# Low-part work of an MLP moved behind the steps of a search, a residual sum by tiles, and a last store in two pieces

## The chip, the cores and the metric

The kernel runs on one core of a Trainium2 chip. The metric is the device time of one execution in microseconds (us). TensorE (PE) does the matmuls and transposes; VectorE (DVE), ScalarE (ACT) and GpSimd (POOL) do the rest; SyncE (SP) issues nearly all DMA transfers. Each engine runs its own instructions in order, and they wait for each other by semaphores.

## The reference

```python
def _L0_cond_ref(emb_s, emb_t, attention_weights, k):
    ...
    att = jax.nn.softmax(attention_weights, axis=-1) * (1.0 / np.sqrt(n).astype(np.float32))
    adj = adj * att
    adj = adj.at[:, diag, diag].set(-jnp.inf)
    _, idx = jax.lax.top_k(flat, k)
    out = jnp.zeros((g, n * n), dtype=adj.dtype).at[rows, idx].set(1.0)
...
def _L1_cond_ref(x, timestep_embed, ada_w, ...):
    ...
    attn_out = attn_out @ out_w + out_b
    x = x + gate1 * attn_out
    x2 = _ln(x) * (1.0 + scale2) + shift2
    h = jax.nn.gelu(x2 @ ffn_w1 + ffn_b1, approximate=False)
    x = x + gate2 * (h @ ffn_w2 + ffn_b2)
    return x
x = x + _L0_cond_ref(fside_BxSx1_0, cond_2048[:, None, :], x, 5120)
x = x + _L1_cond_ref(x, cond_2048, L1_cond_ada_w, ...)
```

x has 4 sequences of 512 rows by 512 columns, in float32. For each, a 0/1 mask of the 5120 largest of 512 x 512 products is added to x; then a transformer block (16 heads of 128, MLP width 2048, modulated by cond) is applied, and its output, which holds x already, is added to x once more. So the result holds the masked x twice.

## The kernel before

Every float32 product is made of three passes with operands split into a high and a low part (`mm3`, lines 1118 to 1120: high by high, high by low, low by high). A tile of MLP-in or a group of four chunks of MLP-out is 12 matmuls of 512 columns. A high part is written by ScalarE, its low part by VectorE.

The four sequences run one after the other. The 5120th largest value of sequence b + 1 is found by bisection while sequence b is computed: 32 steps, each a count by VectorE (`count`, line 803) and one by ScalarE (`topk_count`, line 584) of half the elements, their total by two one-column matmuls of TensorE (`take_total`, lines 1125 and 1126), and the move of the candidate by VectorE (`topk_move`, lines 857 and 860). The search for sequence 0 stands alone at the start; sequence 3 has none beside it. `SLOTS` places the steps: 11 under the heads, 5 under the output projection, then one behind tile 3 of MLP-in and one behind each later tile but tile 12 (11 of them), and the last four at the places (0,0) to (0,3) of MLP-out. At such a place TensorE takes the total (`between`), VectorE makes the step (`step_at`) and ScalarE the next count (`next_count`). (u, r) of MLP-out is unit u, chunks 4r to 4r + 3.

MLP-in has 16 tiles f. The first four are made together in two halves of the rows; from f = 4 on each takes one PSUM bank of seven in turn and waits for the gelu of tile f - 7 (`h_hi`). ScalarE applies the gelu twice (line 751 into `tmp`, which holds four tiles; line 753 into the high part of `act`), and VectorE subtracts (`hidden_lo`, line 995). Before, both loops have, for tile f, first the step of its place, then ScalarE gelu f and VectorE low part f - 1. Unit 0 of MLP-out, which follows, takes the hidden tiles as its 16 chunks and waits for their low parts (`h_lo`): chunk 12 for low parts up to 14, chunk 15 for 15.

VectorE's residual sum `x2 += xm` (line 1062, all four row tiles in one instruction) stands between the second layer norm and the loop of MLP-in. After unit 3 of MLP-out `mlp_add` adds the last column block, and SyncE stores all of `x2` (line 421). Gated outputs of units 1 and 2 (line 990) are transposed by TensorE at place (3,1) (line 1238).

In sequence 0 alone the weights are split too, 40 halves: ScalarE copies the high half (line 622), GpSimd subtracts for the low one (line 514). Both halves of unit 9, which is unit 1 of MLP-out, are copied near the end of MLP-in and in MLP-out, `split_unit(b, 6 + f // 4, 0)` behind gelu 15 and `split_unit(b, 9 + u, 1)` at r = 1. The step at place (0,3) ends with the marks of equal elements (`eqm`, line 874); GpSimd and VectorE then have the splits and the mask (lines 880 to 888) side by side.

Of the kernel before, what the change touches and what calls it, by code (L numbers as in the profile page):

```python
# [40 lines left out]
ALU = mybir.AluOpType  # L41
# [3 lines left out]
P = 128  # L45
# [115 lines left out]
def before_in_place(n, among):  # L161

    return sum(m in among for m in range(n) if PLACE[m] == PLACE[n])


def is_first(b):
# [4 lines left out]
def block_kernel(nc, x, cond, weights, ada_w, cols, out):  # L171
    ctx = ExitStack()
    with ctx:
# [139 lines left out]
        def wait_apart(eng, signal, value):  # L313


            eng.wait_ge(signal, value)
            eng.sem_inc(waits_met, 1)
# [32 lines left out]
        def _(sp):  # L350
# [68 lines left out]
            def store(b):  # L419
                wait_apart(sp, out_ready, b + 1)  # L420
                sp.dma_start(seq(out_seq, b), x2[:, :, :].rearrange("p i d -> p (i d)"))\
                    .then_inc(out_stored, 16)

            def first_sequence():
                load_raw(2, AHEAD + 2)
                wait_apart(sp, xm_ready, 1)
                load_x(1)
                for i in range(DESKS):
                    sp.wait_ge(desk_saved[i], 16 * len(range(i, len(PRE), DESKS)))
                for n in PRE:  # L430
                    if n in (v_half(1, 0), v_half(1, 1)):
                        load_ahead(n, v_done, QUAD)
                load_raw(AHEAD + 2, AT[unit_half(3, 0)])
                wait_apart(sp, pt_done, H * NT)
                load_x_again(1)
                load_raw(AT[unit_half(3, 0)], AT[unit_half(9, 0)] + 2)
                for u in (6, 7, 8):
                    for half in range(2):
                        load_ahead(unit_half(u, half), f_done, 4 * (u - 5))
                load_raw(AT[unit_half(9, 0)] + 2, NHALF)  # L440
                save_split(NHALF - 2)
                save_split(NHALF - 1)
                for place in PLACES:
                    sp.wait_ge(w_saved[place], 16 * w_credit(place))
# [38 lines left out]
            for b in range(1, B - 1):  # L483
                sequence(b)
            sequence(B - 1, last=True)
            store(B - 1)
            sp.wait_ge(out_stored, 16 * B + STORE_CREDIT)


        @block.gpsimd  # L490
# [80 lines left out]
        def _(act_e):  # L571
# [137 lines left out]
            def sequence(b, last=False):  # L709
                split_qk(b, 0)  # L710
                split_qk(b, 1)
                for idx in range(3):
                    v_part(b, idx)
                qk_part(b, 0)

                nc.scalar.activation(table[:, :], ident[:, 0:1], ACT.Exp)
                split_v(b, 1, 0)
                v_part(b, 3)
                for h in range(H):
                    head(b, h, last)  # L720

                def next_count(place):
                    step = SLOTS.get(place)
                    if not last and step is not None:
                        if step + 1 < STEPS:
                            topk_count(b + 1, step + 1)
                        else:
                            topk_sides(b + 1)

                split_unit(b, 2, 0)  # L730
                next_count(("out", 1, 2))
                next_count(("out", 1, 3))
                split_unit(b, 2, 1)
                for r in range(4):
                    if r % 2 == 0:
                        split_unit(b, 3, r // 2)
                    next_count(("out", 2, r))
                split_unit(b, 4)
                ln_root(b * LNS + 1, 0, NT // 2)
                ln_hi(b * LNS + 1, ada2[:, C:2 * C], ada2[:, 2 * C:3 * C], ROWS[0])  # L740
                split_unit(b, 5, 0)
                ln_root(b * LNS + 2, NT // 2, NT)
                ln_hi(b * LNS + 2, ada2[:, C:2 * C], ada2[:, 2 * C:3 * C], ROWS[1])
                split_unit(b, 5, 1)
                for f in range(KC):
                    next_count(("mlp_in", f // 4, f % 4))
                    act_e.wait_ge(f_done, b * KC + (f + 1))
                    if f >= 4:
                        act_e.wait_ge(h_lo, b * KC + (f - 3))
                    bk = bank[BANKS["mlp_in"][f % TURNS]]  # L750
                    nc.scalar.activation(tmp[:, f % 4, :], bk[:, :], ACT.Gelu,
                                         bias=col("b1", f)).then_inc(g_done, 1)
                    nc.scalar.activation(act[:, 0, f, :], bk[:, :], ACT.Gelu,
                                         bias=col("b1", f)).then_inc(h_hi, 1)
                    if f % 4 == 3:
                        split_unit(b, 6 + f // 4, 0)
                    elif f % 4 == 1 and f > 4:
                        split_unit(b, 5 + f // 4, 1)
                for u in range(4):
                    for r in range(4):  # L760
                        next_count(("mlp_out", u, r))
                        if r == 1 and u < 3:
                            split_unit(b, 9 + u, 1)
                        elif r == 3 and u < 2:
                            split_unit(b, 10 + u, 0)
                            if u == 1 and not last:
                                ln_root(b * LNS + LNS)
                        elif not last and (u, r) in ((2, 3), (3, 1)):
                            split_v(b + 1, 0, u - 2)
                if not last:  # L770
                    ln_hi(b * LNS + LNS, ada1[:, 0:C], ada1[:, C:2 * C])
# [24 lines left out]
        def _(dve):  # L796
# [201 lines left out]
            def sequence(b, last=False):  # L998
# [10 lines left out]
                def step_at(place):  # L1009
                    if not last and place in SLOTS:  # L1010
                        topk_step(b + 1, SLOTS[place])
# [17 lines left out]
                def attn_add(u, half=0):  # L1029
# [2 lines left out]
                        return add_back(u, xm)  # L1032
                    return add_back(u, xm, half * NT // 2, (half + 1) * NT // 2)

                def mlp_add(u):
                    dve.wait_ge(y2_back, b * C + (u + 1))
                    return add_back(u, x2)
# [5 lines left out]
                for r in range(4):  # L1043
                    step_at(("out", 2, r))
                    if r in (1, 2):
# [13 lines left out]
                modulate_lo(b * LNS + 1, ROWS[0])  # L1059
                normalise(b * LNS + 2, x2, 1, NT // 2, NT)  # L1060
                modulate_lo(b * LNS + 2, ROWS[1])
                V.tensor_tensor(x2[:, :, :].rearrange("p i d -> p (i d)"),
                                x2[:, :, :].rearrange("p i d -> p (i d)"),
                                xm[:, :, :].rearrange("p i d -> p (i d)"), ALU.add)
                for f in range(KC):
                    step_at(("mlp_in", f // 4, f % 4))
                    if f:
                        hidden_lo(b, f - 1)
                hidden_lo(b, KC - 1)
                for u in range(4):  # L1070
                    for r in range(4):
                        if u and r == 0:
                            mlp_gate(u - 1)
                        step_at(("mlp_out", u, r))
                        if (u, r) == (1, 2):
                            mlp_add(0)
                        if u == 3 and r == 0:
# [360 lines left out]
```

## Time and profile before

| | us |
|---|---|
| median of 3 runs | 1700.54 (1699.61 to 1701.47) |
| profiled execution, its own time | 1700.58 |
| its span, first to last instruction | 1698.7 |
| TensorE busy | 1615.8 (95%) |
| VectorE busy | 1159.3 (68%) |
| ScalarE busy | 856.8 (50%) |
| GpSimd busy | 158.0 (9%) |

Between the span and the execution's time lie 1.9 us. Rows of a timeline give start and duration in us, engine, line, operation, output and inputs, and in brackets the time for which the engine stood before it and what released it. Starts of successive instructions can lie closer than their durations, since an engine's pipeline overlaps them.

### The profile page before, as it was taken

Reading aid. Unit: us, or ns where it says so; the run is one execution under the profiler, and the core shown is the slowest. Engines: PE = TensorE matmul, PEld = TensorE weight load, DVE = VectorE, ACT = ScalarE, POOL = GpSimd, SP = SyncE. Lnnn points to the kernel's source line nnn. Section 1 sums busy time; section 2 is a strip of 40 time slices with the busy share of each in tenths; the row PEclk is TensorE's granted clock in tenths of the full one; section 3 lists DMA queues with packets and bytes.
Section 4 is the critical chain, followed back from the end, with each engine's and each line's share of the span. In section 5 each row is a group of like instructions: output and inputs, shape, how many; then the busy total and the mean of one; then the engine's idle time right before and its main releaser. Section 6 shows DMA issues by size and latency. Waiting matters only on the chain.

```text
span 1698.7 us, 22501 instructions
## 1 busy us (share of the span) xinstructions
PE 1615.8 (95%) x8268; PEld 1354.3 (80%) x8268; DVE 1159.3 (68%) x2524; ACT 856.8 (50%) x1623; POOL 158.0 (9%) x89
## 2 busy tenths in 40 slices
PE   1869999999999999999999999999999999999998
PEld 1758888888788888888778888888878888888887
DVE  6767877767785887776774887776675666665421
ACT  4546666654835455553743555554572445444240
POOL 5511312214040000000000000000000000000000
PEclk9999999999999999999999999999999999999999
DMA  9803525536566232324355232134344331332453
GB/s 373 303 32 124 186 80 180 186 135 251 197 217 236 79 120 101 110 105 157 149 198 221 84 125 114 61 124 149 149 165 186 145 125 50 125 123 85 164 198 124
DMA packets 63853, 256.32 MB, mean 151 GB/s; under 512 B 4352, under 2 KB 4480, under 8 KB 60800
## 3 DMA queue, kind: packets, MB, share of 16 engines
q1 hardware_dynamic: 63456, 254.56, 40.7%
q8 instruction: 66, 1.08, 0.2%
q10 hardware_dynamic: 288, 0.33, 0.1%
q14 instruction: 43, 0.35, 0.1%
HBM read 200.34 MB, written 54.53 MB: 150 GB/s over the span
## 4 chain that ended last, share of the span: by engine, by line
PE 86%; DVE 9%; ACT 3%; issue 1%; DVEq 1%; DMA 0%; SPq 0%; ACTq 0%
PE bank L1118 25%; PE bank L1120 24%; PE bank L1119 24%; PE bank L1212 6%; DVE tb L803 3%; PE bank L1238 1%; PE bank L1280 1%; PE bank L1275 1%; PE bank L1142 1%; PE bank L1276 1%; DVE prob L971 1%; PE bank L1160 1%; ACT prob L679 1%; PE bank L1164 1%; PE bank L1161 1%
## 5 line engine op out<-in xcount | busy, mean ns | idle before, releaser
L1118 PE MATMUL bank<-xT,w 128*128 128x512 f32 x704 | 280.5, 398 | 0.5 <-POOL w L514 0.5
L679 ACT ACTIVATE prob<-bank,nbias 128x512 f32<-128x512 f32 x256 | 176.6, 690 | 201.0 <-DVE nbias L968 201.0
L1120 PE MATMUL bank<-xT,w 128*128 128x512 f32 x704 | 274.8, 390 | 0.0
L1119 PE MATMUL bank<-xT,w 128*128 128x512 f32 x704 | 274.5, 390 | 0.0
L1118 PE MATMUL bank<-act,w 128*128 128x512 f32 (+1 forms) x576 | 217.6, 378 | 0.8 <-DVE act L932 0.8
L1120 PE MATMUL bank<-act,w 128*128 128x512 f32 (+1 forms) x576 | 211.0, 366 | 0.0
L1119 PE MATMUL bank<-act,w 128*128 128x512 f32 (+1 forms) x576 | 210.7, 366 | 0.0
L979 DVE TENSOR_TENSOR probT<-bank,probT 128x512 fp32r<-128x512 f32 x256 | 158.4, 681 | 24.9 <-ACT probT L689 24.8
L962 DVE TENSOR_REDUCE rowmax<-bank 128x1 f32<-128x512 f32 x256 | 174.5, 682 | 0.2 <-issue 0.2
L1120 PEld LDWEIGHTS bank<-xT,w 128*128 128x128 f32 x704 | 132.5, 188 | 27.8
L1118 PEld LDWEIGHTS bank<-xT,w 128*128 128x128 f32 x704 | 132.4, 188 | 25.9 <-POOL w L514 0.9
L1119 PEld LDWEIGHTS bank<-xT,w 128*128 128x128 f32 x704 | 132.8, 189 | 24.9
L689 ACT CAST probT<-bank 128x512 fp32r<-128x512 f32 x256 | 131.0, 604 | 17.6 <-PE bank L1212 17.6
L514 POOL TENSOR_TENSOR w<-wraw,w 128x1024 fp32r<-128x1024 f32 x40 | 103.3, 2587 | 295.5 <-ACT w L622 295.1
L971 DVE TENSOR_SCALAR prob<-prob,rinv 128x512 f32<-128x512 f32 x256 | 125.0, 488 | 5.7 <-issue 0.7
L932 DVE SCALAR_TENSOR_TENSOR act<-bank,small,act 128x512 fp32r<-128x512 f32 x64 | 48.0, 750 | 116.1 <-ACT act L698 116.1
L1212 PEld LDWEIGHTS bank<-ident,prob 128*128 128x128 f32 x1024 | 114.9, 140 | 13.3 <-DVE prob L971 6.2
L1212 PE MATMUL bank<-ident,prob 128*128 128x128 f32 x1024 | 122.7, 273 | 2.6 <-DVE prob L971 2.5
L1120 PEld LDWEIGHTS bank<-act,w 128*128 128x128 f32 x576 | 108.6, 189 | 18.1
L1118 PEld LDWEIGHTS bank<-act,w 128*128 128x128 f32 x576 | 108.6, 189 | 17.7 <-DVE act L932 2.5
L1119 PEld LDWEIGHTS bank<-act,w 128*128 128x128 f32 x576 | 108.8, 189 | 15.3
L932 DVE SCALAR_TENSOR_TENSOR qk<-bank,small,qk 128x512 fp32r<-128x512 f32 x128 | 95.3, 749 | 31.9 <-ACT qk L670 21.3
(136 smaller groups left out, 3040.4 us busy)
## 6 DMA issues: line engine op xcount, KB each, us to landing
w<-split_weights SPq DMA_DIRECT2D x152, 1024.0 KB, 5.3
split_weights<-w SPq DMA_DIRECT2D x40, 1024.0 KB, 6.1
wraw<-weights_in SPq DMA_DIRECT2D x48, 512.0 KB, 4.2
adaw<-ada_w_in SPq DMA_DIRECT2D x4, 1536.0 KB, 15.4
split_weights<-xT SPq DMA_DIRECT2D x6, 1024.0 KB, 7.7
xr<-x_in SPq DMA_DIRECT2D x4, 1024.0 KB, 6.6
out<-x SPq DMA_DIRECT2D x4, 1024.0 KB, 4.4
adj<-x_in SPq DMA_DIRECT2D x3, 1024.0 KB, 6.9
```

The source lines that it names most:

```text
L514: nc.gpsimd.tensor_tensor(w[:, region, 1, span], wraw[:, k % 2, :], w[:, region, 0, span].bitcast(F32), ALU.subtract)\
L679: nc.scalar.activation(prob[:, i, :], bank[i][:, :], ACT.Exp, bias=nbias[:, i:i + 1], scale=SCALE, accum_out=rowsum[:, i:i + 1]).then_inc( ...
L689: nc.scalar.copy(probT[:, 0, j, :], bank[j][:, :]).then_inc(pt_hi, 1)
L803: V.tensor_scalar(passed_v, src, cand[:, :], None, op0=ALU.is_ge, op1=ALU.add, accum_out=cnt_v[:, :]).then_inc(counted_v, 1)
L932: return V.scalar_tensor_tensor(dst, src, bias, hi.bitcast(F32), ALU.add, ALU.subtract)
L962: V.reduce_max(rowmax[:, i:i + 1], bank[i][:, :], AX.X)
L971: V.tensor_scalar(prob[:, i - 1, :], prob[:, i - 1, :], rinv[:, i - 1:i], None, ALU.mult)\
L979: V.tensor_tensor(probT[:, 1, j, :], bank[j][:, :], probT[:, 0, j, :].bitcast(F32), ALU.subtract).then_inc(pt_lo, 1)
L1118: pe.matmul(dst, w_hi_ap, x_hi_ap, start=first, stop=False)
L1119: pe.matmul(dst, w_hi_ap, x_lo_ap, start=False, stop=False)
L1120: return pe.matmul(dst, w_lo_ap, x_hi_ap, start=False, stop=last)
L1212: ins = pe.transpose(bank[j][:, i * P:(i + 1) * P], prob[:, i, j * P:(j + 1) * P], ident[:, :])
```

## The change

The gelus of MLP-in run two places behind the step (`GELU_LAG`), low parts three (`LOW_LAG`); both loops run over into the first places of MLP-out, whose steps they take along. At each place the step stays first. The sum `x2 += xm` becomes four instructions of one row tile, at the places (0,0) to (0,3) of MLP-out, behind the step and ahead of the low part. The store of the last sequence becomes two: the first 384 columns of each row when the additions of units 1 and 2 are done (`y2_added`), the last 128 behind the last addition (`out_ready`).

```diff
+GELU_LAG, LOW_LAG = 2, 3
+def mlp_place(n):
+    return ("mlp_in", n // 4, n % 4) if n < KC else ("mlp_out", 0, n - KC)
...
+            def store_last(signal, columns):
+                wait_apart(sp, signal, B)
+                sp.dma_start(out[B - 1].rearrange("(p i) d -> p i d", p=P)[:, :, columns], x2[:, :, columns])\
+                    .then_inc(out_stored, 16)
...
-            store(B - 1)
-            sp.wait_ge(out_stored, 16 * B + STORE_CREDIT)
+            store_last(y2_added, slice(0, D - P))
+            store_last(out_ready, slice(D - P, D))
+            sp.wait_ge(out_stored, 16 * (B + 1) + STORE_CREDIT)
...
-                for f in range(KC):
-                    next_count(("mlp_in", f // 4, f % 4))
+                for n in range(KC + GELU_LAG):
+                    next_count(mlp_place(n))
+                    f = n - GELU_LAG
+                    if f < 0:
+                        continue
                     act_e.wait_ge(f_done, b * KC + (f + 1))
...
-                        next_count(("mlp_out", u, r))
+                        if 4 * u + r >= GELU_LAG:
+                            next_count(("mlp_out", u, r))
...
+                def add_masked(i):
+                    V.tensor_tensor(x2[:, i, :], x2[:, i, :], xm[:, i, :], ALU.add)
...
-                V.tensor_tensor(x2[:, :, :].rearrange("p i d -> p (i d)"),
-                                x2[:, :, :].rearrange("p i d -> p (i d)"),
-                                xm[:, :, :].rearrange("p i d -> p (i d)"), ALU.add)
-                for f in range(KC):
-                    step_at(("mlp_in", f // 4, f % 4))
-                    if f:
-                        hidden_lo(b, f - 1)
-                hidden_lo(b, KC - 1)
+                for n in range(KC + LOW_LAG):
+                    step_at(mlp_place(n))
+                    if n >= KC:
+                        add_masked(n - KC)
+                    if n >= LOW_LAG:
+                        hidden_lo(b, n - LOW_LAG)
...
-                        step_at(("mlp_out", u, r))
+                        if 4 * u + r >= LOW_LAG:
+                            step_at(("mlp_out", u, r))
+                        if LOW_LAG <= 4 * u + r < NT:
+                            add_masked(r)
```

VectorE from the last low parts of the layer norm (output xT) to the second step of MLP-in, before (a step is three rows: step_up, cand, tb,cnt_v; a low part is act<-tmp,act):

```order
L922 TENSOR_TENSOR xT<-tmp,xT 128x256 x4
L1062 TENSOR_TENSOR x_66<-x_66,xm 128x2048
L995 TENSOR_TENSOR act<-tmp,act 128x512 x2
L857 TENSOR_SCALAR step_up<-bank 128x1
L860 TENSOR_SCALAR cand<-cand,step_up 128x1
L803 TENSOR_SCALAR tb,cnt_v<-low,cand 128x1024
L995 TENSOR_TENSOR act<-tmp,act 128x512
```

The same place after the change:

```order
L941 TENSOR_TENSOR xT<-tmp,xT 128x256 x4
L876 TENSOR_SCALAR step_up<-bank 128x1
L879 TENSOR_SCALAR cand<-cand,step_up 128x1
L822 TENSOR_SCALAR tb,cnt_v<-low,cand 128x1024
L1014 TENSOR_TENSOR act<-tmp,act 128x512
```

The residual sum and two low parts no longer stand ahead of the step.

VectorE at the end of its loop, before: from low parts 14 and 15 to the step at place (0,0) of MLP-out and the next one:

```order
L995 TENSOR_TENSOR act<-tmp,act 128x512 x2
L857 TENSOR_SCALAR step_up<-bank 128x1
L860 TENSOR_SCALAR cand<-cand,step_up 128x1
L803 TENSOR_SCALAR tb,cnt_v<-low,cand 128x1024
L857 TENSOR_SCALAR step_up<-bank 128x1
```

After: the place (0,2), third piece of the sum and low part 15, then the step at (0,3) and the fourth piece:

```order
L876 TENSOR_SCALAR step_up<-bank 128x1
L879 TENSOR_SCALAR cand<-cand,step_up 128x1
L822 TENSOR_SCALAR tb,cnt_v<-low,cand 128x1024
L1056 TENSOR_TENSOR x_66<-x_66,xm 128x512
L1014 TENSOR_TENSOR act<-tmp,act 128x512
L876 TENSOR_SCALAR step_up<-bank 128x1
L879 TENSOR_SCALAR cand<-cand,step_up 128x1
L893 TENSOR_SCALAR eqm,n_eq<-low,cand 128x2048
L1056 TENSOR_TENSOR x_66<-x_66,xm 128x512
L1009 TENSOR_SCALAR yT<-bank,small,ada_77 128x512
```

The last three low parts moved behind the steps of places (0,0) to (0,2), each with a piece of the sum ahead of it.

ScalarE in sequence 0, from gelu 15 to the end of the search, before (passed_s,cnt_s is a count, w<-wraw the copy of a weight half):

```order
L751 ACTIVATE tmp<-bank,small 128x512
L753 ACTIVATE act<-bank,small 128x512
L622 CAST w<-wraw 128x1024
L584 ACTIVATE passed_s,cnt_s<-low,cand 128x1024 x2
L622 CAST w<-wraw 128x1024
L584 ACTIVATE passed_s,cnt_s<-low,cand 128x1024
L591 ACTIVATE signs,sign_sum<-low,cand 128x2048
```

And after:

```order
L769 ACTIVATE tmp<-bank,small 128x512
L771 ACTIVATE act<-bank,small 128x512
L637 CAST w<-wraw 128x1024 x2
L599 ACTIVATE passed_s,cnt_s<-low,cand 128x1024
L606 ACTIVATE signs,sign_sum<-low,cand 128x2048
```

Two counts now come before gelu 15, and the two copies follow it together.

## Rows read from the trace of the kernel before

**Rows 1.** The page: busy time by engine, and the chain's shares.
```profile
PE 1615.8 (95%) x8268; PEld 1354.3 (80%) x8268; DVE 1159.3 (68%) x2524; ACT 856.8 (50%) x1623; POOL 158.0 (9%) x89
...
PE 86%; DVE 9%; ACT 3%; issue 1%; DVEq 1%; DMA 0%; SPq 0%; ACTq 0%
```
**Rows 2.** TensorE's waits over the whole span: total us, times, longest.
```profile
PE bank L1125 <- DVE tb L803: 50.9, 35, 20.9
```
**Rows 3.** Timeline of TensorE, sequence 1, first three takes of MLP-in.
```profile
824.54 0.18 PE L1125 MATMUL bank<-cnt_v,ones 128*128 128x1 f16 x1
...
829.35 0.18 PE L1125 MATMUL bank<-cnt_v,ones 128*128 128x1 f16 x1 [1.72 <-DVE tb L803]
...
832.23 0.18 PE L1125 MATMUL bank<-cnt_v,ones 128*128 128x1 f16 x1
```
**Rows 4.** Timeline of VectorE, the same place.
```profile
822.15 2.29 DVE L1062 TENSOR_TENSOR x<-x,xm 128x2048 f32<-128x2048 f32 x1
...
826.84 0.69 DVE L995 TENSOR_TENSOR act<-tmp,act 128x512 fp32r<-128x512 f32 x1 [0.46 <-ACT act L753]
827.45 0.15 DVE L857 TENSOR_SCALAR step_up<-bank 128x1 f32<-128x1 f32 x1
...
829.21 0.68 DVE L995 TENSOR_TENSOR act<-tmp,act 128x512 fp32r<-128x512 f32 x1
```
**Rows 5.** Timeline of ScalarE, the same place: gelu 1, and the count behind gelu 2.
```profile
825.54 0.69 ACT L751 ACTIVATE tmp<-bank,small 128x512 f32<-128x512 f32 x1
...
827.92 1.15 ACT L584 ACTIVATE passed_s<-low,cand 128x1024 bf16<-128x1024 f32 x1
```
**Rows 6.** Timeline of sequence 1, MLP-out place (0,2): TensorE's take, VectorE's step.
```profile
869.51 0.18 PE L1125 MATMUL bank<-cnt_v,ones 128*128 128x1 f16 x1
...
869.75 0.16 DVE L857 TENSOR_SCALAR step_up<-bank 128x1 f32<-128x1 f32 x1 [1.10 <-PE bank L1126]
```
**Rows 7.** Timeline of sequence 0, start of MLP-in: GpSimd and TensorE.
```profile
427.18 3.89 POOL L514 TENSOR_TENSOR w<-wraw,w 128x1024 fp32r<-128x1024 f32 x1 [6.77 <-ACT w L622]
...
428.92 0.18 PE L1125 MATMUL bank<-cnt_v,ones 128*128 128x1 f16 x1
...
431.11 0.50 PE L1118 MATMUL bank<-xT,w 128*128 128x512 f32 x1 [0.48 <-POOL w L514]
...
434.03 0.18 PE L1125 MATMUL bank<-cnt_v,ones 128*128 128x1 f16 x1 [1.26 <-DVE tb L803]
```
**Rows 8.** Timeline of sequence 0: first copy of ScalarE, second split of GpSimd for unit 9.
```profile
468.50 1.04 ACT L622 CAST w<-wraw 128x1024 fp32r<-128x1024 f32 x1
...
474.22 2.40 POOL L514 TENSOR_TENSOR w<-wraw,w 128x1024 fp32r<-128x1024 f32 x1 [2.18 <-ACT w L622]
```
**Rows 9.** Timeline of GpSimd and VectorE, sequence 0; VectorE's same line in sequence 1.
```profile
483.26 8.79 POOL L514 TENSOR_TENSOR w<-wraw,w 128x1024 fp32r<-128x1024 f32 x2 [6.64 <-ACT w L622]
...
485.66 4.13 DVE L886 SCALAR_TENSOR_TENSOR eqm<-adj,need,low 128x2048 bf16<-128x2048 f32 x1 [0.15 <-issue]
...
881.06 2.35 DVE L886 SCALAR_TENSOR_TENSOR eqm<-adj,need,low 128x2048 bf16<-128x2048 f32 x1 [0.15 <-issue]
```
**Rows 10.** Timeline: gates and transposes of units 1 and 2, sequence 0; additions, sequence 1.
```profile
503.64 1.53 DVE L990 TENSOR_SCALAR yT<-bank,small,ada 128x512 f32<-128x512 f32 x2
...
505.02 1.03 PE L1238 MATMUL bank<-ident,yT 128*128 128x128 f32 x8
...
901.06 1.28 DVE L1025 TENSOR_TENSOR x<-x,bank 128x512 f32<-128x512 f32 x2 [5.06 <-PE bank L1238]
```
**Rows 11.** Transfers (count, KB each, us to landing): last store, a load, a small one.
```profile
out<-x SPq DMA_DIRECT2D x1, 1024.0 KB, 3.9
...
w<-split_weights SPq DMA_DIRECT2D x1, 1024.0 KB, 5.2
...
small<-cols_in ACTq DMA_DIRECT2D x1, 64.0 KB, 1.9
```
**Rows 12.** Stretch of sequence 2: busy by engine, then TensorE's granted clock, DMA share.
```profile
1226.00:1230.00 4.00, 4.00 (x14) 2.89 (x13) 2.17 (x6) 2.44 (x5) 0.00 (x0) 0.57 0.41 167
```

## The prediction

> **What bounds the kernel now.** I read the shares of busy time and the chain of work that ended last first: TensorE is busy 95% of the span and carries 86% of the chain [rows 1]. So a change pays only where TensorE stands still, and the table of its waits says where. 50.9 us of them are waits for VectorE's count, but 35 waits with one of 20.9 us among them [rows 2]: 32 belong to the search ahead of sequence 0, which nothing here touches. The other three are one per sequence but the last, all at the same place, the second search step of MLP-in [rows 3]. Sequence 3 has no search beside it and no such wait. After the last matmul the output store stands alone.
>
> In [rows 3] the three takes of a total stand at 824.54, 829.35 and 832.23 us. The second interval is 2.88 us, and the 13 other takes of this stage have no wait: 2.87 us is a tile of 12 matmuls and a take. The first is 4.81 us, so 1.94 us too long. Why is in [rows 4]: VectorE first adds xm to x2 (2.29 us from 822.15), then makes low parts 0 and 1 as ScalarE's gelus allow, and starts the step at 827.45, though its total was asked for at 824.54. The count ends at 829.3 and TensorE goes on at 829.35.
>
> **Part 1, the search step first.** From the prices of [rows 4]: a low part occupies VectorE 0.61 us (826.84 to 827.45) and is finished after 0.69; a step occupies it 1.76 us (827.45 to 829.21), and the count is out 0.09 later. A step starts 0.24 us after the take [rows 6]. So after the change the count is out 0.24 + 1.76 + 0.09 = 2.1 us after the take, with 2.87 to spare. The gelus of two tiles occupy ScalarE from 825.54 to 827.92 at most, 1.19 us a tile; a count takes 1.15 and begins 0.47 after its step [rows 4, 5]. With gelu 0 behind it it counts from 825.5 to 826.8, before 827.4 too. The wait goes: 1.94 us in sequences 1 and 2. What was queued behind the step is late by less than a tile: gelu f runs two tiles later, but a bank of MLP-in is taken again only seven tiles on, and tmp holds four tiles. Through the rest of MLP-in a VectorE tile costs 1.76 + 0.61 = 2.37 us of 2.87 and a ScalarE tile 1.15 + 1.19 = 2.34, so both still keep up.
>
> In sequence 0 the same place reads 428.92 to 434.03, 5.11 us [rows 7], since 0.5 us more went to a wait for a weight half that GpSimd split in 3.89 us. It takes 2.40 elsewhere [rows 8], and it was held up by the addition that is taken away. Started at 427.18 it ends at 429.6 without it, ahead of its use near 430.5. Removed there: 5.11 - 2.87 = 2.24 us.
>
> **Part 2, what now comes in MLP-out.** This is a new wait, and no row of before shows it. The tiles 16 to 18 of VectorE's loop now hold a step, a piece of the residual sum and a low part: 1.76 + 0.61 + 0.61 = 2.98 us (the piece, two SBUF operands of 128x512, is taken at the price of a low part) against TensorE's 2.87. TensorE needs low part 14 for chunk 12 of unit 0 and low part 15 for chunk 15. Call the take of place (0,1) t. VectorE is 0.24 + 2.98 - 2.87 = 0.35 behind it when it starts. Low part 14 is out at t + 0.35 + 2.37 + 0.69 = 3.41, plus some 0.05 for the signal; TensorE is ready for chunk 12 at t + 2.87 + 0.15 = 3.02. Wait: about 0.4 us. VectorE is free at t + 0.35 + 2.98 = 3.33, so low part 15 is out at 3.33 + 2.37 + 0.69 + 0.05 = 6.44; TensorE, with 9 matmuls at 0.227 behind it (2.04), stands ready at 3.46 + 2.04 = 5.5. Wait: about 0.93. Together 1.33 us per sequence. Bounds: nothing, if the pieces cost far less than a low part, and 2.2 if each costs half as much again. So sequences 1 and 2 gain 1.94 - 1.33 = 0.61 each, 1.2 us in all, most of the saving being given back 40 us later.
>
> **Part 3, sequence 0 pays more.** ScalarE also writes the high half of split weights there, and the order shows both copies for unit 9 behind gelu 15. They were some 4.6 us apart, the first at 468.50 and the second ahead of the split at 474.22 [rows 8], at times when VectorE had only steps. Now they follow gelu 15: with t as above ScalarE begins its count at t + 0.24 + 0.47 = 0.71, ends it at 1.87, ends gelu 15 at 3.06, copies for 1.04 until 4.1, and GpSimd splits from 4.2 to 6.6 (2.40), then wants the next half. VectorE wants its third piece of the sum at 3.33 + 1.76 = 5.1. The trace shows what then happens [rows 9]: a VectorE instruction with two SBUF inputs took 4.13 us instead of 2.35, since it stood until GpSimd's first split was through; two splits took 8.79 us instead of 4.8, since the second stood until VectorE was through. They go one at a time and alternate. So the piece runs from 6.6 to 7.3, GpSimd's second split, its copy done at 5.2, from there to 9.7, and low part 15 from 9.7 to 10.4. TensorE waits for it from 5.5 to 10.4: 4.9 us in place of 0.93.
> This agrees with the Trainium skill, SBUF — State Buffer, section "Who interferes with whom": one port pair is shared by VectorE and GpSimd, exclusively, and the second to issue is blocked. By that rule a count with an accumulator is not blocked, which holds here too; who is served next when both have one queued it does not tell.
>
> The step's last count then leads to the chain that ends in the gates of units 1 and 2. It gets the fourth piece, 0.6 us. In sequence 0 the pair of gates occupies VectorE from 503.64 to 505.17, and TensorE transposes the first from 505.02, the second after four of 0.11 us, at 505.46 [rows 10]: 0.3 us of slack at the second, so 0.6 late costs 0.37 with the signal. In sequence 1 VectorE then stands 5.06 us until those transposes are through [rows 10], and sequence 2 repeats that: 0.6 late costs nothing. Sequence 0: -2.24 + 0.40 + 4.92 + 0.37 = +3.45 us.
>
> **Part 4, the residual sum and the last store.** Moving the 2.29 us itself costs nothing beyond the above; in sequence 3, without steps, VectorE has the time for its pieces. The last store now has only a quarter of its bytes behind the last addition, but in 512 pieces of 512 B where there were 128 pieces of 8 KB. Rows near it [rows 11]: 1 MB in 128 pieces landed in 3.9 us; a load of 1 MB in 256 pieces in 5.2, so 1.3 for 128 pieces more; 64 KB in 128 pieces in 1.9. The last gives the lower end, 2.0 us gained; the middle one the upper, 3.9 + 3 x 1.3 - 2.0 for the bytes gone = 5.8, 1.9 lost. The load's bytes are not fewer, so its rate of pieces may be that of memory; I take 3.2 us, nearer to the small transfer, a gain of 0.7. The larger store may start after place (3,1), with two groups of chunks (2 x 2.72) and the last addition still to come, and is gone by then.
> By the Trainium skill, DMA: Bandwidth & Descriptors, section "Anatomy of one DMA — SWDGE (gpsimd) path", a transfer costs 2.0 us and its bytes at 436 GB/s, 2.6 us here and 1.8 less than for four times the bytes; the sum would be 1.1 us lower by it. No row shows that for pieces this small.
>
> **Sum.** +3.45 - 1.2 - 0.7 = +1.5 us on the profiled execution's 1700.58, which is the median of the runs (1700.54): **1702.1 us**, inside the 0.2% (3.4 us, the bounds 1697.1 and 1703.9) that a measurement of this kernel can tell from no change.
>
> **The rivals.**
> A, VectorE keeps the port for its next instruction. Low part 15 was issued while the piece was under way, and no row shows two such VectorE instructions back to back with a split waiting. Then low part 15 is out at t + 7.9, the wait is 2.4 instead of 4.9, and the sum 1699.6.
> B, no collision: GpSimd's splits fall elsewhere, because a copy waits for a transfer or the pieces come earlier. Then sequence 0 is at -2.24 + 1.33 + 0.37 = -0.54 and the time 1698.1. Against it speaks that both raw halves were in place before.
> C, the slower side: the clock. After the 1.94 us too much in sequence 2 the granted clock was 0.57 of full speed over 4 us, part of it at 1.2 GHz [rows 12]: 4 x 0.43 = 1.7 us. A stop of 4.9 us in sequence 0 is over twice as long. If it brings such a fall and the one in sequence 2 stays, the time is 1703.8 to 1704; with a store at its upper bound it would be 1706.4. It decides from the point at which a stop of some five microseconds lowers the clock. For it: the fall came right after a stop of TensorE. Against: the same 1.94 us in sequence 1 brought none, and if stops bring falls, the one in sequence 2 should go with its stop, which cancels.
> D, the whole does more than it says: B, the fall in sequence 2 gone (1.7), the store at its lower bound: 1695.1.
>
> **How the numbers follow.** Forecast 0.4, A 0.28, B 0.17, C 0.1, D 0.05. Only D ends below 1697.1, so faster 0.05. Slower gets 0.11: most of C, and the forecast with a last store at its upper bound (1704.7). The rest, 0.84, is within 0.2%. The range, 1697.0 to 1704.0, takes in the forecast, A, all but the last of B's lower bound (1696.8), and the near end of C; outside it lie D and the slow stores, under 0.2 together.
>
> **What would show it.** TensorE's waits for the count shrink by 4.7 us (1.26 + 1.72 + 1.72) and to 32; in sequences 1 and 2 two new waits on low parts (about 0.4 and 0.9 us) stand in unit 0 of MLP-out. In sequence 0 the second is 4.9 us, with a piece of the sum and a low part each over 2 us long. The transposes of units 1 and 2 wait some 0.4 us there. From the last addition to the span's end 0.7 us less. Wrong would be: no wait at chunk 15 (pieces are cheap), no long low part in sequence 0, or a take that still waits in MLP-in, which would mean that ScalarE's count and not VectorE's was late.

## The result, and the profile after

The changed kernel takes 1703.7 us (median of 21 runs, 1701.0 to 1705.4) beside 1700.5 for the kernel before (21 runs, 1698.9 to 1702.2). The ratio is 1.0018, 95% interval 1.0011 to 1.0024: slightly slower, at the edge of what this measurement tells from no change. The profiled execution took 1705.4 us, its span 1703.7.

The page of the changed kernel, busy time by engine and the shares of the chain, reads almost as in [rows 1]:

```profile
PE 1618.4 (95%) x8268; PEld 1354.7 (80%) x8268; DVE 1165.6 (68%) x2536; ACT 856.4 (50%) x1623; POOL 157.6 (9%) x89
...
PE 85%; DVE 10%; ACT 3%; issue 1%; DVEq 1%; DMA 1%; POOL 0%; SPq 0%; ACTq 0%
```

TensorE's waits over the whole span (total us, times, longest):

```profile
PE bank L1149 <- DVE tb L822: 48.2, 32, 20.5
...
PE bank L1142 <- DVE act L1014: 6.5, 6, 4.2
```

Against [rows 2] the three waits for the count in MLP-in are gone (35 to 32 times), and six new ones on low parts have come. The total fell by 2.7 us only, since waits in the search ahead of sequence 0, which the change doesn't touch, came out 2 us longer; more on that below. The takes of sequence 1, to be read against [rows 3] (timeline of TensorE: start, duration):

```profile
833.08 0.18 PE L1149 MATMUL bank<-cnt_v,ones 128*128 128x1 f16 x1
...
836.02 0.18 PE L1149 MATMUL bank<-cnt_v,ones 128*128 128x1 f16 x1
...
838.89 0.18 PE L1149 MATMUL bank<-cnt_v,ones 128*128 128x1 f16 x1
```

The first interval is 2.94 us where it was 4.81: 1.87 gained. Later in the same sequence, in unit 0 of MLP-out, TensorE now waits twice for a low part, at chunks 12 and 15 (its timeline):

```profile
876.66 0.50 PE L1142 MATMUL bank<-act,w 128*128 128x512 f32 x1 [0.37 <-DVE act L1014]
...
879.63 0.50 PE L1142 MATMUL bank<-act,w 128*128 128x512 f32 x1 [0.60 <-DVE act L1014]
```

The same place of sequence 0 is worse (timeline of all engines, 475 to 484 us):

```profile
475.27 1.99 ACT L637 CAST w<-wraw 128x1024 fp32r<-128x1024 f32 x2
...
475.61 0.50 PE L1142 MATMUL bank<-act,w 128*128 128x512 f32 x1 [0.37 <-DVE act L1014]
...
476.38 5.14 POOL L529 TENSOR_TENSOR w<-wraw,w 128x1024 fp32r<-128x1024 f32 x2 [43.83 <-ACT w L637]
...
477.23 2.09 DVE L1056 TENSOR_TENSOR x<-x,xm 128x512 f32<-128x512 f32 x1
...
477.56 0.40 PE L1144 MATMUL bank<-act,w 128*128 128x512 f32 x1
...
479.25 2.82 DVE L1014 TENSOR_TENSOR act<-tmp,act 128x512 fp32r<-128x512 f32 x1
...
482.12 0.79 PE L1142 MATMUL bank<-act,w 128*128 128x512 f32 x1 [4.16 <-DVE act L1014]
...
482.71 0.63 PE L1143 MATMUL bank<-act,w 128*128 128x512 f32 x1
483.14 0.63 PE L1144 MATMUL bank<-act,w 128*128 128x512 f32 x1
```

ScalarE's two copies stand together, so GpSimd has two splits to do from 476.38. The piece of the sum (L1056), 0.69 us elsewhere, takes 2.09, low part 15 (L1014) 2.82, and TensorE, ready at 477.8, starts chunk 15 at 482.12. The matmuls behind it then start 0.43 us apart, not 0.23. The reason stands in the stretches (length, busy of PE, PEld, DVE, ACT, POOL, then TensorE's granted clock):

```profile
477.00:482.00 5.00, 0.96 (x5) 0.44 (x3) 5.00 (x4) 1.40 (x3) 4.52 (x2) 0.87 0.37 122
482.00:490.00 8.00, 7.88 (x25) 6.05 (x26) 5.92 (x9) 5.31 (x6) 0.10 (x1) 0.65 0.81 317
490.00:496.00 6.00, 6.00 (x33) 4.79 (x32) 5.84 (x3) 0.78 (x1) 6.00 (x2) 1.00 0.04 6
```

From 480.7 the clock was at its lower level, 1.2 GHz, for 6.8 us, and TensorE had stood still for 3 us when it fell. In sequences 1 and 2 the two waits on low parts add to 1.0 us in each.

The end of the span (transfers of the last 5.7 us: KB each, us from issue to landing), where [rows 11] had 1024 KB and 3.9:

```profile
out<-x SPq DMA_DIRECT2D x1, 256.0 KB, 2.6
```

### The profile page after: what moved, and what is told of

Read it like the earlier page. It is cut to its first block, busy times and chain, and to the rows that moved or that the text cites. A ratio compares the mean times of both kernels' runs of the same rounds, so it can differ in the third digit from the quotient of the medians.

```text
span 1703.7 us, 22515 instructions
## 1 busy us (share of the span) xinstructions
PE 1618.4 (95%) x8268; PEld 1354.7 (80%) x8268; DVE 1165.6 (68%) x2536; ACT 856.4 (50%) x1623; POOL 157.6 (9%) x89
## 4 chain that ended last, share of the span: by engine, by line
PE 85%; DVE 10%; ACT 3%; issue 1%; DVEq 1%; DMA 1%; POOL 0%; SPq 0%; ACTq 0%
PE bank L1142 24%; PE bank L1144 24%; PE bank L1143 24%; PE bank L1236 6%; DVE tb L822 3%; PE bank L1304 1%; PE bank L1262 1%; PE bank L1299 1%; PE bank L1166 1%; PE bank L1300 1%; DVE prob L990 1%; PE bank L1184 1%; ACT prob L694 1%; PE bank L1188 1%; PE bank L1185 1%
```

## The experiments

A shift below is the start of one and the same matmul in two traces, compared; a stop is given by the distance of two matmul starts, 0.23 us where nothing waits. The traces also differ where their programs are the same: by up to 2.2 us in the search ahead of sequence 0 and by up to 1.4 us in its heads. So shifts are taken between places behind both.

**1. The store alone.** The kernel before with the two-piece last store:

```diff
-            store(B - 1)
+            store_last(y2_added, slice(0, D - P))
+            store_last(out_ready, slice(D - P, D))
```

> The kernel before with the last store in two pieces and nothing else. In the changed kernel the last store (256 KB) landed in 2.6 us, where 1 MB had taken 3.9. Theory (the tail is worth what the shorter landing says, and acts alone): 1.2 to 1.3 us less, 1699.3. Rival (the larger store delays something, or the saving needs the rest): within 0.3 us of 1700.5. Of the clock nothing changes.

Measured: 1698.8 us (11 runs; before beside it 1700.8), ratio 0.9992, interval 0.9984 to 1.0001. The transfer again takes 2.6 us, and the ends of the two traces stand 1.3 us nearer to their last matmul. The gain of 1.3 is real; the medians agree with it but couldn't have shown it alone.

**2. Lags with the sum where it was.** The changed kernel, with the sum as one addition ahead of MLP-in:

```diff
+                V.tensor_tensor(x2[...], x2[...], xm[...], ALU.add)
                 for n in range(KC + LOW_LAG):
                     step_at(mlp_place(n))
-                    if n >= KC:
-                        add_masked(n - KC)
```

> The changed kernel with the residual sum back in one instruction ahead of MLP-in; both lags and the store stay. Theory (the pieces of the sum are what makes VectorE late in MLP-out, 2.98 us a tile against 2.87): the step of MLP-in stays free of a wait in sequences 1 and 2, the wait at chunk 12 goes, the one at chunk 15 falls from 0.77 to about 0.55; in sequence 0 the second split no longer comes between, so that TensorE waits about 2.3 us at chunk 15 instead of 4.4, but the weight half waits for GpSimd again (0.6). In all about 1697 without a fall of the clock, 1698.5 with one. Rival (the lag of three itself is too long): the waits at chunk 15 stay as they are, and the time is 1702 to 1703.

Measured: 1699.8 us, ratio 0.9995 (0.9986 to 1.0004). The stops of MLP-in are gone as in the changed kernel (1.87 us in sequences 1 and 2). With no piece ahead of it, low part 15 meets only the first split (timeline of VectorE, sequence 0):

```profile
477.52 2.18 DVE L1014 TENSOR_TENSOR act<-tmp,act 128x512 fp32r<-128x512 f32 x1
```

The distance at chunk 15 is 2.28 us instead of 4.56, and in sequences 1 and 2 it is 0.79 instead of 0.99, with no wait at chunk 12. So the pieces are what makes the waits in MLP-out large, while the lag of low part 15 alone still leaves a stop of 0.55 us (a shift of 0.73 over unit 0). The old place of the sum keeps its price in sequence 0: the split at the start of MLP-in is late and TensorE waits there (0.88 between two starts). Its trace has 3.4 us at the low clock; for that case 1698.5 was expected, and the time came out 1.3 us above it.

**3. The second copy further behind.** The copy for unit 9's second half one place later, behind the count:

```diff
-                        if r == 1 and u < 3:
+                        if r == (1 if u else 2) and u < 3:
```

> The changed kernel with ScalarE's second copy of unit 9 moved one place, behind the count of place (0,2). Theory (VectorE and GpSimd take turns, and the second split of GpSimd came in ahead of low part 15): GpSimd has one split to do then, low part 15 follows the third piece of the sum at once, and the wait at chunk 15 of sequence 0 falls from 4.4 to about 2.4 us. Time 1701.6, and 1699 to 1700 if the fall of the clock goes as well. Rival (low part 15 is late because of the first split alone, or of the count): the wait stays above 4 us and the time at 1703.7.

Measured: 1703.2 us, ratio 1.0015 (1.0006 to 1.0024), and the distance at chunk 15 is 4.56 again, with VectorE rows of 2.09 and 2.82. The change missed its aim: the copy moved by 1.1 us only and was done before the first split ended, so both splits were queued as before. It tells nothing about the turns; it does show that the order of this copy and the count behind it makes no difference.

**4. TensorE kept busy.** The changed kernel, with 18 idle matmuls into a free bank ahead of chunk 15 in sequence 0:

```diff
+                    if is_first(b) and phase == "mlp_out" and u == 0 and kc == KC - 1:
+                        for _ in range(18):
+                            pe.matmul(bank[1][:, :], w[:, 0, 0, 0:P], act[:, 0, 0, :], start=True, stop=True)
```

> The changed kernel, in sequence 0 alone with 18 more matmuls of 512 columns (4.1 us) ahead of chunk 15 of unit 0, into a bank that nobody reads: TensorE works through the stop of 4.4 us. Theory (the stop makes the clock fall to 1.2 GHz for 6.8 us, which costs 2.6 us): the granted clock stays full there, low part 15 is still out at the same time, and the time is 2.6 us less, 1701.1. Rival (the fall has nothing to do with the stop): it stays, and the time is 1703.7 or up to 0.3 more.

Measured: 1701.9 us, ratio 1.0006 (0.9997 to 1.0015), against 1.0018 without the filler. VectorE's rows at that place are 2.12 and 2.88 us, so the stop of the real work is the same, but the clock stays whole behind it (stretches, last but two the granted clock):

```profile
476.00:482.00 6.00, 5.82 (x28) 4.32 (x26) 5.07 (x4) 1.32 (x3) 4.52 (x2) 1.00 0.50 177
482.00:490.00 8.00, 8.00 (x41) 6.47 (x41) 7.55 (x8) 6.08 (x6) 1.80 (x1) 1.00 0.67 261
```

From place 470 to 520 us of the kernel before, the real work is 5.2 us later here and 7.5 in the changed kernel: the low clock cost 2.3 us. Work that computes nothing made the kernel some 2 us faster; the two intervals overlap a little, and it is the traces that carry the figure.

**5. One split at a time.** The second copy waits for low part 15, in sequence 0 only:

```diff
-                        if r == 1 and u < 3:
+                        if r == (1 if u else 2) and u < 3:
+                            if is_first(b) and u == 0:
+                                act_e.wait_ge(h_lo, b * KC + KC)
```

> The changed kernel, with one wait more in sequence 0: ScalarE's copy for the second half of unit 9 stands behind its count of place (0,2) and waits until low part 15 is out. So GpSimd has only one split to do while VectorE works on the third piece of the sum and low part 15; the second follows both. Theory (port turns: the first split blocks the piece, the second gets in ahead of low part 15): the piece still ends with the first split, but low part 15 now follows it at once in 0.7 us, and the stop of TensorE at chunk 15 of unit 0 shrinks from 4.3 us to about 2.2 (a distance of 2.4 between the two matmul starts instead of 4.56). Rival (ScalarE and gelu 15 are late anyway, or the first split alone costs it all): the distance stays at 4.5. Since sequence 0 is then 2.1 us shorter, and a fall of the clock behind the stop gets rarer or shorter (3.4 us of it cost 1.6, 6.8 us 2.6), I expect 1700.3 to 1701, a ratio of about 1.000 against 1.0018 of the changed kernel.

Measured: 1699.6 us (before beside it 1700.6), ratio 0.9997 (0.9988 to 1.0005); the distance at chunk 15 is 2.42 us. VectorE in its timeline, then GpSimd:

```profile
474.59 2.09 DVE L1058 TENSOR_TENSOR x<-x,xm 128x512 f32<-128x512 f32 x1
476.60 0.68 DVE L1016 TENSOR_TENSOR act<-tmp,act 128x512 fp32r<-128x512 f32 x1
```
```profile
473.75 2.38 POOL L529 TENSOR_TENSOR w<-wraw,w 128x1024 fp32r<-128x1024 f32 x1 [43.77 <-ACT w L637]
478.44 2.38 POOL L529 TENSOR_TENSOR w<-wraw,w 128x1024 fp32r<-128x1024 f32 x1 [2.31 <-ACT w L637]
```

The piece still stands until the first split is through; low part 15 now takes 0.68 us instead of 2.82. The second split was worth 2.1 us. This experiment also moved the copy behind the count, as in experiment 3, where that changed nothing: the two engines do take turns. The time is 0.7 us below what was expected, although the clock fell for 3.4 us behind this shorter stop too.

**6. Pieces without lags.** The kernel before, its one sum replaced by a piece in each of the places (0,0) to (0,3):

```diff
-                V.tensor_tensor(x2[...], x2[...], xm[...], ALU.add)
...
                         step_at(("mlp_out", u, r))
+                        if u == 0:
+                            add_masked(r)
```

> The kernel before, with one part of the change alone: the residual sum is no longer one addition ahead of MLP-in but four pieces, one in each of the places (0,0) to (0,3) of MLP-out, behind the step. Gelus, low parts and counts keep the order of before, and so does the one store. Theory: the pieces cost something only together with low parts that are late. Here low part 15 is made before place (0,0), so no wait at chunks 12 and 15 of unit 0. In MLP-in VectorE is free 2.3 us earlier, but gelus 0 and 1 and their low parts still stand ahead of the second step, so the stop there (4.81 between two takes, 2.87 without a stop) shrinks only by what the sum held back: low parts 0 and 1 follow the gelus, not the sum, and 1.9 stays within 0.3. In sequence 0 GpSimd's split at 427 us takes about 2.4 instead of 3.89 and the wait of 0.5 us for the weights goes. Total: -0.6 us to -1.0 against before, 1699.8, ratio 0.9995. Rival (the sum itself makes the stop in MLP-in): the stops of 1.94 us go here too, and the time is 1695.

Measured: 1702.6 us, ratio 1.0013 (1.0005 to 1.0022), 2.8 us above the expectation. The mechanism held: the stops of MLP-in stand at 2.11 us in all three sequences, as before, so it is the order of step and low parts that makes them, not the sum, and there is no wait on a low part in MLP-out. But the first stop is followed by the low clock here (438.2 us on, 3.4 us), as it was in sequence 2 of the kernel before; and two pieces of sequence 0 meet a split (timeline of VectorE):

```profile
475.63 1.57 DVE L1037 TENSOR_TENSOR x<-x,xm 128x512 f32<-128x512 f32 x1
...
481.24 1.59 DVE L1037 TENSOR_TENSOR x<-x,xm 128x512 f32<-128x512 f32 x1
```

which makes the steps behind them late. By the shifts TensorE loses 1.0 us from there to the transposes of the gates (0.3 at the take of (0,1), 0.35 at 493.8 us, 0.3 at the transposes) and 0.3 more in what follows. The gain at the start of MLP-in was 0.3, not 0.6. That adds to +1.0 us. The other 0.9 us of the median were not traced to a cause; the low clock, worth 1.6 us in this trace, would be enough if it comes more often there.

**7. Catching up in tile 12.** Gelus trail by two and low parts by three only up to place (3,0), which has no step; there two of each are made, and from there gelus trail by one and low parts by two. Two pieces of the sum stand in (3,0), two in (0,2) and (0,3):

```diff
+                    for f in ([n - 3] if n < CATCH_UP else [n - 3, n - 2] if n == CATCH_UP else [n - 2]):
+                        if f >= 0:
+                            hidden_lo(b, f)
+                    if n == CATCH_UP:
+                        add_masked(0)
+                        add_masked(1)
...
+                    if f == KC - 1:
+                        split_unit(b, 9, 0)
```

> A third version. Gelus trail by two tiles and low parts by three only up to tile 12, the place without a step: there gelus 10 and 11 and low parts 9 and 10 are made, and from there gelus trail by one tile and low parts by two, so that gelu 15 stands in place (0,0) and low part 15 in (0,1). Of the sum two pieces stand in place (3,0) and two in (0,2) and (0,3). The copies of unit 8 are behind gelus 12 and 14, the first of unit 9 ahead of gelu 15. The store in two pieces as in the changed kernel. Theory: the stops in MLP-in are gone (-1.94 in sequences 1 and 2, -2.24 in 0), low parts 14 and 15 are out a tile earlier, at t+2.6 and t+6.1 with t the take of (0,1) less a tile, before chunk 12 (5.9) and chunk 15 (7.9) want them, so no stop in MLP-out, and none to bring the clock down; the end is 1.25 shorter. Sum: -7.4 us, 1693 to 1695, ratio 0.9960 (0.9967 if the clock falls once). Rival (something else, ScalarE's total work or the weights, sets the pace there and each microsecond saved is lost at the next place): ratio 0.999 to 1.000.

Measured: 1694.0 us (6 runs; before 1700.6), ratio 0.9966 (0.9954 to 0.9978), within the expectation. No wait of MLP-in or of unit 0 is left, and the clock stays whole over the place of the collision (stretch of sequence 0):

```profile
470.00:490.00 20.00, 20.00 (x98) 15.85 (x97) 18.72 (x23) 11.67 (x16) 11.50 (x4) 1.00 0.47 168
```

TensorE is busy all 20 us. Shifts against the second trace of the kernel before: -2.16 us at the second take of sequence 0, -1.88 and -1.87 in sequences 1 and 2. This version beats both kernels. It changes three things together, the trailing of low parts, the places of the pieces and those of ScalarE's copies, and no run tells apart what each is worth; in sequences 1 and 2, which have no copies, the first two alone leave unit 0 without a wait.

**8. Low part ahead of the piece.** The changed kernel, two statements exchanged:

```diff
-                    if n >= KC:
-                        add_masked(n - KC)
                     if n >= LOW_LAG:
                         hidden_lo(b, n - LOW_LAG)
+                    if n >= KC:
+                        add_masked(n - KC)
```

> The changed kernel, with the order of two instructions exchanged: in places (0,0) and (0,1) of MLP-out the low part stands ahead of the piece of the sum, not behind it (in (0,2) they stood so already in effect after the step: there too the low part now comes first). Theory: each piece costs VectorE 0.6 us ahead of a low part. In sequences 1 and 2 the wait at chunk 12 (0.3 us) goes, and of the 0.77 at chunk 15 about 0.3 to 0.5 goes, since one piece fewer stands ahead of low part 15. In sequence 0 nothing much changes (4.3 us at chunk 15), because the piece of (0,1) is still ahead and the two splits still take their turns: 4.0 to 4.5. Sum: -1.3 us at most against the changed kernel, 1702.2, ratio 1.0012. Rival (the order of pieces is without effect, the gelus are late): 1.0018 as the changed kernel.

Measured: 1698.9 us, ratio 0.9991 (0.9982 to 1.0), against 1.0018 for the changed kernel: some 4.6 us less. I had expected 1702.2. In sequence 0 the low part now takes the turn behind the first split, and the piece, for which nobody waits, the long one (timeline of VectorE):

```profile
476.01 2.08 DVE L1014 TENSOR_TENSOR act<-tmp,act 128x512 fp32r<-128x512 f32 x1
478.02 2.87 DVE L1056 TENSOR_TENSOR x<-x,xm 128x512 f32<-128x512 f32 x1
```

The distance at chunk 15 is 2.37 us and the clock doesn't fall. My expectation had kept a piece ahead of low part 15 where the exchange had just removed it; the rule of turns was right and my bookkeeping of the queue wrong. In sequences 1 and 2 unit 0 is 0.6 us shorter, one piece, but all of it at chunk 12: the distance at chunk 15 stays at 0.97, since TensorE also gets there earlier. New is a wait of 0.98 us for the second split of unit 9 at 491.85, which the long stop had hidden.

**9. Both kernels again.** Unchanged, for further traces.

> The kernel before, unchanged, for a second trace of it. Two things stand in one trace only so far. In the search ahead of sequence 0 the interval between takes 16 and 17 was 6.05 us in before and 8.35 in the changed kernel; if that is by the landing time of a raw weight half (run to run) and not by the change, a second trace of the same program may show either of about 6.1 and 8.3. And the clock: in the first trace no fall after the stops of sequences 0 and 1, and 3.4 us at half clock after that of sequence 2 (cost 1.6). If a stop of 2 us brings a fall only sometimes, it stands elsewhere or not at all here; if the place decides, it is at sequence 2 again.

> The changed kernel, unchanged, for a second trace of it. Fixed by the program, so the same again: 4.56 us between two matmul starts at chunk 15 in sequence 0 with VectorE rows of 2.1 and 2.8 us, 0.53 and 0.99 in sequences 1 and 2. Of the clock: if a stop of 4.3 us brings a fall every time, half clock stands behind it again (6.8 us in the first trace, 3.4 in that of the kernel with the second copy moved); if it is chance, one of the two new traces has none. Interval between takes 16 and 17: 6.1 or 8.3 us, by run.

> The changed kernel, unchanged, for a third trace, with the same expectations as the second: 4.56, 0.53, 0.99 us between matmul starts again; half clock behind the stop in sequence 0 if the stop of 4.3 us brings it every time; 6.1 or 8.3 us between takes 16 and 17 by run.

The three took 1698.5, 1706.0 and 1702.8 us (one run each). The stops are fixed by the program: 4.56 and 4.53 us at chunk 15, 0.53 and 0.54 at chunk 12. Two things are not. The kernel before has no low clock in sequence 2 this time (stretch; compare 0.57 in [rows 12]):

```profile
1225.00:1229.50 4.50, 4.50 (x22) 3.55 (x22) 3.89 (x9) 4.21 (x9) 0.00 (x0) 1.00 0.51 210
```

and between places 1225 and 1232 us its two traces part by 1.6 us. The changed kernel has the low clock behind its stop in every trace, for 3.4 us in the second and 6.8 in the third. And the search ahead of sequence 0 has its 8.3 us in the second trace and 6.1 in the third, so that is of the run. VectorE there in the changed kernel's first trace:

```profile
54.08 2.91 DVE L885 TENSOR_SCALAR low<-adj,cand 128x2048 f32<-128x2048 uint16 x1
57.07 2.96 DVE L888 TENSOR_TENSOR low<-low,adj 128x2048 f32<-128x2048 f32 x1
```

and in its third:

```profile
54.22 1.29 DVE L885 TENSOR_SCALAR low<-adj,cand 128x2048 f32<-128x2048 uint16 x1
55.58 2.29 DVE L888 TENSOR_TENSOR low<-low,adj 128x2048 f32<-128x2048 f32 x1
```

GpSimd, which makes both halves there, begins on a weight half as its transfer lands; its subtraction starts at 53.57 in the first and at 51.80 in the third. The same collision as in sequence 0 costs 2.2 us or nothing.

## Why the prediction was right in its range, and where it was not

The forecast was 1702.1 us, measured were 1703.7, inside the range by 0.3 us. The sign and most terms of the program were right, the clock was not: the time is that of rival C (1703.8), and that the range took it in owes something to luck. The terms against the traces (shifts against the second trace of the kernel before, which has neither low clock nor a slow search):

| term | predicted | measured |
|---|---|---|
| second step of MLP-in, sequence 0 | -2.24 | -2.16 |
| the same, sequences 1 and 2 | -1.94 each | -1.87 each |
| unit 0, chunks 12 and 15, sequences 1 and 2 | +1.33 each | +1.50 and +1.53 |
| unit 0, sequence 0, clock whole (experiment 4) | +5.32 | +5.10 |
| gates of units 1 and 2, sequence 0 | +0.37 | under 0.1 |
| last store | -0.7 | -1.3 |
| clock behind the stop | 0 | +1.5 to +2.9 |

**Part 1** held in every number. The waits for the count are gone, and nothing else in MLP-in became late except once: a weight half that comes by transfer, at 445 us, holds TensorE for 0.4 to 0.9 us in four traces of kernels that get there earlier, and not in the others. The prediction had asked what is late next, and had not looked at that transfer.

**Part 2** held: two waits where it put them, 0.4 and 0.9 predicted; the rows of sequence 1 show 0.37 and 0.60, and the shifts 1.5 in all, since the matmuls behind each stop also start a little further apart. Most of the gain is given back 40 us later: 1.87 against 1.5. Experiments 2 and 8 show the two halves of its reckoning: one piece is worth 0.6, the lag alone 0.7 (shifts over unit 0).

**Part 3** was the part on which the sign hung, and its mechanism is shown, not only argued: the piece 2.09, low part 15 2.82, the splits 5.14 together, and with the second split taken away (experiment 5) 2.1 us less. Rival A, VectorE keeping its turn, is out: low part 15 was queued and had to stand. Rival B is out too, both halves were there. The Trainium skill (SBUF — State Buffer, "Who interferes with whom") says that the port pair is locked exclusively and the second is blocked; the trace agrees, and adds that after each instruction the other engine is served if it has one ready. The 0.37 at the gates did not come. That step took the fourth piece as 0.6 us late for the gates, but by then TensorE was itself later than in the reckoning, by its stop and, where it fell, the clock; experiment 4, without the low clock, has 0.05 there too. The other traces fit that: where TensorE is less late there, the transposes do lose time, 0.3 us in experiment 6 and 0.4 in experiment 8.

**Part 4** had the mechanism right and the size off: I took 3.2 us for the transfer, between bounds of 1.9 and 5.8, and it took 2.6. The row of the load, with its 1.3 us for 128 more pieces, was a poor neighbour. The one sentence on the Trainium skill (DMA: Bandwidth & Descriptors, "Anatomy of one DMA — SWDGE (gpsimd) path") gave an estimate of 2.6, and the trace agrees for this store, which SyncE issues. For the gain it gave 1.8 us and the traces show 1.3: by its figures the 1 MB store would take 4.4 us, and it took 3.9.

**The clock** is the step that failed. Rival C said that a stop of 4.9 us brings a fall, gave 1703.8 and got a chance of 0.1. It is what happened: the fall came in four of four traces with that stop (6.8, 3.4, 6.8 us, and 3.4 in experiment 3), and experiment 4, which fills the stop, is 2 us faster and has none. I argued against it from two stops of 1.94 us of which one brought a fall. That was evidence for about one in two at that length, and should have weighed more for twice the length. All traces together: after stops of 4.5 us the clock fell 4 times in 4; after stops of 2.1 us 2 times in 9; after 2.3 to 2.4 us 2 times in 3. The price was 1.5 to 1.9 us for 3.4 us at 1.2 GHz and 2.3 to 2.9 for 6.8, part of which falls into the stop itself.

**The sum.** The program's terms, as measured, add to -2.16 + 5.10 + 0.05 - 1.87 + 1.50 - 1.87 + 1.53 - 1.3 = +1.0 us, and some 0.3 of small shifts that no row names, most of it in sequence 3; +1.5 was predicted. Experiment 4, the same program with the clock kept up, was measured at +1.1. The medians of the two kernels differ by 3.2. The clock makes up the rest, 1.5 to 2.9 in every trace of the changed kernel, against 1.6 in one of two traces of the kernel before.

## What to carry to other kernels

Where work is made to trail so that a wait goes away, it must catch up before somebody needs the last of it: at a place with spare time, not behind the loop. Here that, with the pieces and copies placed to suit it, turned +3.2 us into -6.6. Where two engines share a port, look at what stands first in the queue when the other's long instruction ends, and put there what TensorE waits for; an exchange of two statements was worth 4.6 us.

## What the runs showed of the hardware

- VectorE and GpSimd took turns on instructions with two SBUF inputs: 0.69 us of VectorE's work became 2.09, the next 2.82, while each split of 2.4 us ran whole. A count of VectorE ran on undisturbed beside a split (1.28 us from 476.02, with the split from 476.38). A conversion with one input (L885) is held up too, 1.29 to 2.91 us.
- A stretch at 1.2 GHz followed 4 of the 12 stops whose distance of starts was 2.1 to 2.4 us, and 4 of 4 at 4.5 us, all four at one place of the program; it was 3.4 or 6.8 us long. It makes two traces of one and the same program differ by 1.6 us.
- 256 KB in 512 pieces of 512 B landed in 2.6 us, 1 MB in 128 pieces in 3.9. What the pieces cost by themselves was not tested apart.
